# A head projection with even and odd columns crossed, so that one projection serves both halves of the rotary turn

## The reference

```python
qkv = x @ qkv_w + qkv_b                    # 16 heads of 64, for q, k and v
def rot(t):                                # rotary turn of q and k, in pairs of columns
    t = t.reshape(*t.shape[:-1], half, 2)
    t0, t1 = t[..., 0], t[..., 1]          # even and odd columns
    r0 = t0 * cos - t1 * sin
    r1 = t1 * cos + t0 * sin
    return jnp.stack([r0, r1], axis=-1).reshape(*t0.shape[:-1], head_dim)
attn = softmax(einsum('bhqd,bhkd->bhqk', rot(q), rot(k)) / sqrt(64))
out = einsum('bhqk,bhkd->bhqd', attn, v) ... @ out_w + out_b
```

## Time and profile before

| | |
|---|---|
| executions | 1848.84, 1851.65, 1853.36 us (median 1851.65) |
| profiled execution | its span is 1847.4 us; the profile gives no other time of its own |
| median less that span | 4.25 us |
| PE, POOL, DVE, ACT busy | 94%, 77%, 78%, 76% of the span |

### The profile page before, as it was taken

How to read it: one execution, slowest core, us unless ns; L and a number is a source line. 1 busy time by engine, 2 the same in 40 slices (tenths; PEclk the granted TensorE clock), 3 DMA queues, 4 the chain that set the end, 5 groups by cost and what they waited for, 6 DMA issues and landing times. The chain is left out here.

```text
span 1847.4 us, 53971 instructions
## 1 busy us (share of the span) xinstructions
PE 1740.1 (94%) x22856; PEld 1101.7 (60%) x22856; DVE 1444.6 (78%) x2658; ACT 1407.5 (76%) x1737; POOL 1430.4 (77%) x851
## 2 busy tenths in 40 slices
PE   5999999999999999999999999986899999978997
PEld 2466666666666666666666666675556666653454
DVE  5888888888888888888888887535988888845785
ACT  2688888888888888888888888943998888853463
POOL 6699999999999999999999999974765566624122
PEclk9899999999999999999999999998999999989998
DMA  5101010111101010101010010050111111110000
GB/s 142 25 20 31 19 31 23 27 26 28 26 24 30 21 31 19 31 23 28 23 31 23 24 26 4 2 165 18 41 40 36 37 37 37 34 26 1 1 0 24
DMA packets 71080, 56.89 MB, mean 31 GB/s; under 512 B 29196, under 2 KB 64184, under 8 KB 70840
## 3 DMA queue, kind: packets, MB, share of 16 engines
q1 hardware_dynamic: 70840, 53.44, 11.5%
HBM read 14.54 MB, written 1.05 MB: 8 GB/s over the span
## 5 line engine op out<-in xcount | busy, mean ns | idle before, releaser
L278 POOL TENSOR_TENSOR ah_probs_lo<-ah_probs,ah_probs_hi 128x1024 f16<-128x1024 f32 x512 | 1072.8, 2132 | 78.8 <-ACT ah_probs L487 78.7
L542 DVE TENSOR_REDUCE ah_part_max<-ah_p_m 128x1 f32<-128x512 f32 x1024 | 669.2, 685 | 120.9 <-PE ah_p_m L342 111.1
L484 ACT ACTIVATE ah_probs_hi<-ah_p_s 128x1024 f16<-128x1024 f32 x512 | 531.2, 1038 | 190.0 <-PE ah_p_s L358 178.8
L487 ACT ACTIVATE ah_probs<-ah_p_s 128x1024 f32<-128x1024 f32 x512 | 532.4, 1040 | 0.0
L372 PE MATMUL ah_p_o<-ah_v_hi,ah_probs_hi 128*128 128x65 f16 x4096 | 470.5, 195 | 5.7 <-POOL ah_probs_lo L278 5.1
L374 PE MATMUL ah_p_o<-ah_v_lo,ah_probs_hi 128*128 128x64 f16 x4096 | 470.5, 193 | 0.0
L376 PE MATMUL ah_p_o<-ah_v_hi,ah_probs_lo 128*128 128x65 f16 x4096 | 470.3, 194 | 0.0
L372 PEld LDWEIGHTS ah_p_o<-ah_v_hi,ah_probs_hi 128*128 128x128 f16 x4096 | 383.0, 98 | 84.3 <-DVE a_attn L565 12.3
L374 PEld LDWEIGHTS ah_p_o<-ah_v_lo,ah_probs_hi 128*128 128x128 f16 x4096 | 378.4, 98 | 91.3
L342 PE MATMUL ah_p_m<-ah_k_hi_lo,ah_q_hi_twice 128*128 128x512 f16 x1024 | 393.9, 385 | 6.6 <-DMA ah_max_q_lo<-ah_lo 3.1
L357 PE MATMUL ah_p_s<-ah_q_hi_twice,ah_k_hi_lo 128*128 128x512 f16 x1024 | 388.6, 379 | 0.8 <-ACT ah_probs L487 0.4
(11 more groups left out here) (316 smaller groups left out, 3090.0 us busy)
## 6 DMA issues: line engine op xcount, KB each, us to landing
ba_v_skew<-ba_v_own SPq DMA_DIRECT2D x64, 129.0 KB, 2.3
ah_q_hi_twice<-ah_hi SPq DMA_DIRECT2D x128, 64.0 KB, 2.0
ah_k_hi_lo<-ah_hi SPq DMA_DIRECT2D x64, 64.0 KB, 1.9
ah_one_k_hi<-ah_hi SPq DMA_DIRECT2D x64, 64.0 KB, 2.0
ah_k_hi_lo<-ah_lo SPq DMA_DIRECT2D x64, 64.0 KB, 2.0
ah_max_q_lo<-ah_lo SPq DMA_DIRECT2D x64, 64.0 KB, 2.0
ah_w_head<-in_w_heads SPq DMA_DIRECT2D x16, 160.0 KB, 2.4
bw_rot<-in_rot SPq DMA_DIRECT2D x4, 512.0 KB, 10.3
```

Of the source, the lines that this page charges most:

```text
L278: pool.tensor_tensor(pl[:, p % RW, :, :], pb[:, p % RP, :, :], ph[:, p % RW, :, :], ALU.subtract).then_inc(lo_pool, 1)
L484: act.activation(ph[:, p % RW, :, :], p_s[:, p % 2, :, :], ACT.Exp, scale=HD ** -0.5)
L487: act.activation(pb[:, p % RP, :, :], p_s[:, p % 2, :, :], ACT.Exp, scale=HD ** -0.5).then_inc(exp_done, 1)
L542: dve.tensor_reduce(part[:, t, 2 * half + b:2 * half + b + 1], p_m[:, b, :], AX, ALU.max).then_inc(maxed, 1)
```

## The change

In the steady turns q and k are projected once. The columns of a head are put in the order even q, odd k, odd q, even k, in four blocks of 32 rows (`QE`, `KO`, `QO`, `KE`). What an even column needs from its odd partner then stands 64 rows away. DVE multiplies by the sine table into `rot_sin` (`cross_sin`) and by the cosine table in place (`cross_cos`), and adds across: rows 0 to 63 of the bank get rows 64 to 127 of `rot_sin` (`cross_first`), and rows 64 to 127 get minus rows 0 to 63 (`cross_second`). Both are of 64 rows by 512 columns. The order on DVE changes: the sine goes behind both reductions of j = 0, the cosine stays between those of j = 1, `cross_first` goes behind them, and `cross_second` goes behind the reductions of j = 2.

The transfers take blocks of 32 rows: eight of `hi` and four of `lo` in a turn, for four and two. A head's weights have 448 columns in the first two heads (the lead turns still use both old layouts) and 192 in the others, for 320.

```diff
-W_COLS = 5 * HD
-W_TURNED, W_QK, W_V = slice(2 * HD, 4 * HD), slice(0, 2 * HD), slice(4 * HD, 5 * HD)
+QUAD = HD // 2
+W_COLS, W_LATER = 7 * HD, 3 * HD
+W_CROSSED, W_V, W_QK, W_TURNED = (slice(0, 2 * HD), slice(2 * HD, 3 * HD), slice(3 * HD, 5 * HD),
+                                  slice(5 * HD, 7 * HD))
+QE, KO, QO, KE = (slice(i * QUAD, (i + 1) * QUAD) for i in range(4))
...
-        SPREAD = 6 * 16
+        SPREAD, SPREAD_CROSSED = 6 * 16, 12 * 16
...
+        def w_cols(h):
+            return slice(0, W_COLS if h < 2 else W_LATER)
...
+                    if g >= LEAD_G:
+                        sp.dma_start(ka[0:QUAD, to, cs], hi[KE, g % 2, :]).then_inc(spread[g % 2], 16)
+                        sp.dma_start(ka[QUAD:HD, to, cs], hi[KO, g % 2, :]).then_inc(spread[g % 2], 16)
+                        sp.dma_start(kb[HD:HD + QUAD, to, cs], hi[KE, g % 2, :]).then_inc(spread[g % 2], 16)
+                        sp.dma_start(kb[HD + QUAD:P, to, cs], hi[KO, g % 2, :]).then_inc(spread[g % 2], 16)
+                        for half in range(2):
+                            at = half * HD
+                            sp.dma_start(qa[at:at + QUAD, to, cs], hi[QE, g % 2, :]).then_inc(spread[g % 2], 16)
+                            sp.dma_start(qa[at + QUAD:at + HD, to, cs], hi[QO, g % 2, :]).then_inc(spread[g % 2], 16)
+                        sp.wait_ge(lo_done, g + 1)
+                        sp.dma_start(ka[HD:HD + QUAD, to, cs], lo[KE, g % 2, :]).then_inc(spread[g % 2], 16)
+                        sp.dma_start(ka[HD + QUAD:P, to, cs], lo[KO, g % 2, :]).then_inc(spread[g % 2], 16)
+                        sp.dma_start(qb[HD:HD + QUAD, to, cs], lo[QE, g % 2, :]).then_inc(spread[g % 2], 16)
+                        sp.dma_start(qb[HD + QUAD:P, to, cs], lo[QO, g % 2, :]).then_inc(spread[g % 2], 16)
+                        continue
...
                     if j == 0 and g <= LAST_G:
                         pe.wait_ge(vl_done, g)
-                        project(turned_bank(g), g, W_TURNED, turned_ready)
-                    if j == 1 and g <= LAST_G:
-                        pe.wait_ge(rot_done, g + 1)
-                        project(proj_bank(g), g, W_QK, proj_ready)
+                        project(proj_bank(g), g, W_CROSSED, proj_ready)
...
+                def cross_sin(g):
+                    h = g // QC
+                    dve.wait_ge(proj_ready, g + 1)
+                    dve.wait_ge(r_done, g)
+                    dve.wait_ge(first_half, g - LEAD_G)
+                    dve.scalar_tensor_tensor(rot[:, :], p_a[:, :], bqk[:, 2, h:h + 1], sin[:, chunk(g % QC)], ALU.add,
+                                             ALU.mult).then_inc(rot_done, 1)
+
+                def cross_cos(g):
+                    h = g // QC
+                    dve.wait_ge(rot_done, g + 1)
+                    dve.scalar_tensor_tensor(p_a[:, :], p_a[:, :], bqk[:, 2, h:h + 1], cos[:, chunk(g % QC)], ALU.add,
+                                             ALU.mult).then_inc(cos_done, 1)
+
+                def cross_first(g):
+                    dve.wait_ge(cos_done, g + 1)
+                    dve.tensor_tensor(p_a[0:HD, :], p_a[0:HD, :], rot[HD:P, :], ALU.add).then_inc(first_half, 1)
+
+                def cross_second(g):
+                    dve.wait_ge(cos_done, g + 1)
+                    dve.tensor_tensor(p_a[HD:P, :], p_a[HD:P, :], rot[0:HD, :], ALU.subtract).then_inc(r_done, 1)
...
                     if g <= LAST_G:
-                        if j == 0:
-                            rotate_sin(g)
                         if j == 1:
-                            rotate_cos(g)
-                        if j == 2:
-                            rotate_sum(g)
+                            cross_cos(g)
                         if j == 4:
                             low(g)
...
                     if g <= LAST_G:
+                        if j == 0:
+                            cross_sin(g)
+                        if j == 1:
+                            cross_first(g)
+                        if j == 2:
+                            cross_second(g)
                         if j == 3:
                             high(g)
```

More of the change, by code:

```diff
@@ L147, in mha_heads @@
         wl = sc.sb("w_lo", [P, 2, W_COLS], F16)
-        bqk = sc.sb("bias_qk", [P, 2, HEADS])
+        bqk = sc.sb("bias_qk", [P, 3, HEADS])
         qa = sc.sb("q_hi_twice", [P, SETS, S], F16)
@@ L173, in mha_heads @@
         (ident_in, w_in, bias_in, x_turned, xh_ready, xl_ready, v_ones, zeroed, consts, w_hi_done,
-         w_split, turned_ready, proj_ready, rot_done, cos_done, r_done, hi_done, lo_done, v_ready, vh_done,
+         w_split, first_half, turned_ready, proj_ready, rot_done, cos_done, r_done, hi_done, lo_done, v_ready, vh_done,
          vl_done, m_ready, maxed, m_done, m_turned, mrow_ready, s_ready, exp_done, lo_pool, o_ready, rcp_done,
@@ L177, in mha_heads @@
              "ident_in", "w_in", "bias_in", "x_turned", "xh_ready", "xl_ready", "v_ones", "zeroed", "consts",
-             "w_hi_done", "w_split", "turned_ready", "proj_ready", "rot_done", "cos_done", "r_done",
+             "w_hi_done", "w_split", "first_half", "turned_ready", "proj_ready", "rot_done", "cos_done", "r_done",
              "hi_done", "lo_done", "v_ready", "vh_done", "vl_done", "m_ready", "maxed", "m_done", "m_turned",
@@ L184, in mha_heads, with spread_after @@
         spread = [sc.sem(f"spread{b}") for b in range(2)]
-        SPREAD = 6 * 16
+        SPREAD, SPREAD_CROSSED = 6 * 16, 12 * 16
         LAST_G = TURNS - 1
+        def spread_after(turns):
+            early = min(turns, LEAD_G // 2)
+            return SPREAD * early + SPREAD_CROSSED * (turns - early)
+        def w_cols(h):
+            return slice(0, W_COLS if h < 2 else W_LATER)
         def turned_bank(g):
@@ L222, in _ @@
                         sp.wait_ge(w_split, h + 1)
-                        sp.dma_start(w32[:, :], a["w_heads"][h + 1]).then_inc(w_in, 16)
+                        sp.dma_start(w32[:, w_cols(h + 1)], a["w_heads"][h + 1, :, w_cols(h + 1)]).then_inc(w_in, 16)
                     sp.wait_ge(hi_done, g + 1)
+                    if g >= LEAD_G:
[13 more added lines that the diff above has]
+                        continue
                     sp.dma_start(ka[0:HD, to, cs], hi[HD:P, g % 2, :]).then_inc(spread[g % 2], 16)
@@ L238, in split_weights @@
                         pool.wait_ge(v_ready, QC * (h - 1))
-                    pool.tensor_copy(wh[:, h % 2, :], w32[:, :]).then_inc(w_hi_done, 1)
+                    cols = w_cols(h)
+                    pool.tensor_copy(wh[:, h % 2, cols], w32[:, cols]).then_inc(w_hi_done, 1)
                     pool.wait_ge(w_hi_done, h + 1)
-                    pool.tensor_tensor(wl[:, h % 2, :], w32[:, :], wh[:, h % 2, :], ALU.subtract).then_inc(w_split, 1)
+                    pool.tensor_tensor(wl[:, h % 2, cols], w32[:, cols], wh[:, h % 2, cols],
+                                       ALU.subtract).then_inc(w_split, 1)
                 split_weights(0)
@@ L266, in _ @@
                     pool.wait_ge(hi_done, g + 1)
-                    pool.wait_ge(spread[g % 2], SPREAD * (g // 2))
+                    pool.wait_ge(spread[g % 2], spread_after(g // 2))
                     pool.tensor_tensor(lo[:, g % 2, :], pb[:, g - BY_DVE, 1, :], hi[:, g % 2, :],
@@ L337, in maxima @@
                         for b in range(2):
-                            pe.wait_ge(spread[b], SPREAD * QC // 2 * (n + 1))
+                            pe.wait_ge(spread[b], spread_after(QC // 2 * (n + 1)))
                     for b in halves:
@@ L444, in high @@
                     if g >= 2:
-                        act.wait_ge(spread[g % 2], SPREAD * (g // 2))
+                        act.wait_ge(spread[g % 2], spread_after(g // 2))
                     rotated = proj_bank(g) if g < BY_DVE else pb[:, g - BY_DVE, 1, :]
@@ L514, in high @@
                     dve.wait_ge(r_done, g + 1)
-                    dve.wait_ge(spread[g % 2], SPREAD * (g // 2))
+                    dve.wait_ge(first_half, g - LEAD_G + 1)
+                    dve.wait_ge(spread[g % 2], spread_after(g // 2))
                     dve.tensor_copy(hi[:, g % 2, :], proj_bank(g)).then_inc(hi_done, 1)
@@ L2296, in _layouts @@
     turned = np.roll(order, HD // 2)
-    a["w_heads"] = c(np.concatenate([w[:, 0][..., order], w[:, 1][..., order], w[:, 0][..., turned],
-                                     w[:, 1][..., turned], w[:, 2]], -1).transpose(1, 0, 2))
+    even, odd = order[:HD // 2], order[HD // 2:]
+    crossed = lambda q, k: np.concatenate([q[..., even], k[..., odd], q[..., odd], k[..., even]], -1)
+    a["w_heads"] = c(np.concatenate([crossed(w[:, 0], w[:, 1]), w[:, 2], w[:, 0][..., order], w[:, 1][..., order],
+                                     w[:, 0][..., turned], w[:, 1][..., turned]], -1).transpose(1, 0, 2))
     b = i["L0_attn_qkv_b"].reshape(3, HEADS, HD)
```

(3 more changed lines are left out.)

## The result

The changed kernel takes 1863.95 us (median of 4, 1859.65 to 1865.89), the kernel before 1851.34 beside it (median of 4). The ratio is 1.0077, 95% interval 1.0057 to 1.0096: slower by 0.8%, 12.6 us. The profiled execution's span is 1862.1, 14.7 above that of before.

The account below looks back on a forecast made before the run. PE sets the pace with VectorE right behind, and VectorE becomes the bound: span 1847.4 + 4.6 (longer turns) + 0.5 (start-up) = 1852.5, with 4.25 to the median 1856.8 us; range 1835 to 1866, likeliest 1853 to 1860.

Parts of the forecast that it names:

- What bounds: Steps 1 to 5 of a steady turn: VectorE becomes the bound, leaving only 0.26 us of PE's saving.
- PE's 0.645 and 0.14 us: PE, each steady turn: three projection matmuls fewer save 0.645 us, and a stall in step 3 of 0.14 goes.
- The chain: VectorE from step 1's first reduction to the start of step 4's half 1 reduction: 8.02 us without late starts.
- The late starts: VectorE, four instructions at row-half changes: each starts at its predecessor's end, costing 0.085 us, 0.34 a turn.
- the rival of free row changes: VectorE's four row-half changes cost nothing: a turn of 17.94 us, 1837.1 us in all; chance 0.33.
- the upper bound from the rows: VectorE's four row-half changes start 0.03 after the predecessor's end: 0.12 each, 0.48 a turn, 1864.8 us; rival's chance 0.15.
- The sum: Whole kernel: span 1847.4 + 4.6 + 0.5 = 1852.5 us, with 4.25 to the median 1856.8.
- the 4.25 from span to median: Whole kernel: the 4.25 us between the earlier kernel's profiled span and its median, added to the forecast span.
- Start-up: First two heads: 448 weight columns for 320 lengthen each split by 0.50 us; +0.5 taken, from 0 to 1.0.
- Transfers and POOL: Steady turns: twelve transfer issues take 7.2 us and POOL at most 17.5, both hidden; late transfer queue 54 us, chance 0.02.

Follow-up runs that it names:

- the version with the early cosine: Changed kernel with the cosine multiplication moved to directly behind the sine in step 0; 1818.9 us, ratio 0.9834 to the kernel before.
- the version at row 0: Changed kernel with both 64-row additions working on rows 0 to 63 alone, so part of the computation differs; 1835.18 us, ratio 0.9927 to the kernel before.
- the swapped pair: Changed kernel with `cross_second` first and `cross_first` directly behind it, both behind the reductions of step 1; 1862.22 us, ratio 1.0064 to the kernel before.
- the split sum: Kernel before with its one sum of 128 rows split into two of 64 rows, upper rows first; 1893.81 us, ratio 1.0248.

## Why the prediction was nearly right, point by point

**What bounds, right.** The prediction said that PE's 0.645 and 0.14 us would be taken back because VectorE becomes the bound of steps 1 to 5. It does, in the stalls of 0.39 and 0.59 above, and the version with the early cosine shows it by undoing it: PE's work is the same, VectorE's chain is shorter, and 45 us go.

**The chain, right to 0.01.** By its rows it was 8.02 us without late starts. In the version at row 0, which has none, it runs from 705.08 to 713.09, 8.01, and a turn takes 17.94: the prediction named 17.94 for that case. Its median is 1835.18, beside 1837.1 for the rival.

**The late starts, right in place, mis-sized.** All four stand where the prediction put them, and with them the forecast and not the rival of free row changes. The term that failed is their price. I took 0.085 each, a start at the predecessor's end; measured are 0.12, 0.11, 0.11 and 0.14 against 0.60, 0.48 together, for the 0.34. That is the upper bound from the rows (0.48, a start 0.03 behind the end), which stood among the rivals with 1864.8 and 0.15. The measured time, 1863.95, is in the range stated but outside the 1853 to 1860 of the forecast, which had 0.40. That it comes so near to the rival's 1864.8 is in part luck, as the next points show: a turn grew by 0.25 and not by 0.22, and smaller terms went the other way. The argument by which I took the middle, that there is no data to wait for on top, has fallen. The 0.02 above 0.12 in the last of them is the upper rows' addition, which lasts 0.71; the prediction had said that it would be wrong if such an addition lasted other than 0.69, and in this small part it was.

Which instructions would start late was an estimate of mine too, as no row of before has a change of start row. The runs show the late starts in each place tried: four in the changed kernel (0.71 and 0.72 behind reductions, 0.74 behind `cross_second`), none with both additions at row 0, two with the swapped pair (0.72 and 0.74) with the cosine on time (0.61), and two with the split sum, where nothing crosses. Such an instruction starts 0.03 us after the end of the one ahead, and 0.01 after it on the way back to row 0 with the split sum.

**The sum.** From half 0 of step 1 to half 1 of step 5 the forecast had 706.26 - 696.74 = 9.52, measured is 9.69: 0.14 from the late starts, 0.03 from the rest of the chain (713.36 - 704.83 = 8.53, less 0.48, is 8.05 for 8.02). So a turn grew by 0.25 and not by 0.08. 58 x 0.17 = 9.9 us were missing, and the median came out 7.2 above the 1856.8. Two things went the other way. One is the start, below. The other is the 4.25 from span to median: the changed kernel's median is only 1.85 above its profiled span. In nearly all executions on record the device time is about 2 us over the span of the same execution, so some 2.4 of the 4.25 most likely came from a profiled execution of the kernel before that was one of its quick ones, and did not belong in the sum.

**Start-up, wrong in sign, small.** I added 0.5. The third start of the beat is at 86.6 where before it is at 87.6, though the second of the two turns ahead of it is 0.25 longer. So the first turn of the loop got shorter by some 1.2 us (from its first start to its second 19.1 for 20.3), and the 0.5 is not to be seen; no run took apart why.

**Transfers and POOL, right.** With six transfers nothing changes. POOL is not in the way at 18.45; at 17.42 it is, by 0.16 in one turn of four.

**What the prediction did not see.** It forecast a slower turn from a chain in which the cosine had kept its old place. That place was forced in the kernel before by the second projection, and with that projection gone it was free to move into 0.69 us of idle time. And it treated the chain to the second gate as the only one; in the changed kernel that gives the right sum, but not in versions that move work across the first.

## What to carry to other kernels

When work is taken off the leading engine, write down the other engine's chain by starts, instruction by instruction, up to each place where it lets the leader go on; each such place is a gate of its own, and the time lost at an early one did not come back here (the 1.01 in step 3 of the swapped version). A wait that goes also frees the order: look for the idle time that it leaves, and put the work there (here one instruction, 45 us). Keep VectorE's instructions at one start row, or group those at another row; each switch between rows 0 and 64 cost 0.11 to 0.14 us in the traces here.

## What the runs showed of the hardware that I had not expected

- In a row of VectorE instructions that all start at row 0 the next one starts 0.08 us before the end of the one ahead (0.60 behind a reduction of 0.68). Where the start changed between rows 0 and 64 it came 0.01 to 0.03 after that end. One that waits for the result of the one ahead starts 0.03 after it too (in the early-cosine version the cosine starts 0.78 behind a sine of 0.75). So a change of rows cost about as much here (0.11 to 0.14) as this dependency (0.11, by the 0.67 after which the next instruction follows a sine of 0.75 in the earlier trace rows).
- It is tied to the start row, not to crossing. A row of an SBUF input is enough: `cross_first` has only `rot_sin` at row 64 and started 0.71 behind its reduction, and 0.60 with that at row 0 too. And it shows on the cosine, though its operands and those of the reduction ahead of it all start at row 0: it starts 0.72 behind that reduction in the changed kernel, where the last addition, some 14 us earlier, is the one at row 64; 0.61 and 0.60 in the swapped and the row-0 version, where the last addition is at row 0. No run took apart what in that addition makes the cosine late.
- A 64-row addition at row 64 lasts 0.71 us in every turn, one at row 0 0.68 or 0.69, and the sum of 128 rows in the kernel before 0.69.
